# A graph network's aggregations: TensorE's counts raised by a drain instead of by the last product

## The chip, the cores and the metric

The kernel runs on one core of a Trainium2 chip. The metric is the device time of one execution in microseconds, without a profiler; three executions are listed, and their median counts. A profile is one further execution that the hardware profiler recorded.

## The reference, cut to what matters

Two layers of a graph network run over 6,250 nodes with 256 features and 100,000 edges that are sorted by destination. Layer 0 sums weighted neighbour rows, adds a linear attention, and ends in a routed feed-forward block of 32 experts. Layer 1 does two graph convolutions, a second mixer and a block with 64 slices in 8 heads. Everything is float32. The part that the change sits in is the neighbour sum, which is computed three times:

```python
msgs = edge_vals[:, None] * x[edge_src]
agg = jax.ops.segment_sum(msgs, edge_dst, num_segments=N)
# and twice, in the two convolutions of layer 1:
agg = jax.ops.segment_sum(norm[:, None] * xW[src], dst, num_segments=n_nodes)
```

## The kernel before, in words

**Stages.** The program runs stage after stage: setup, a front that normalises the rows, a first aggregation, two dense stages, routing with its experts, a second front, a second and a third aggregation, a small stage over heads and an output stage. In each stage every engine runs its own written-out list of instructions, and engines wait for one another by counts on semaphores.

**An aggregation** (`stage_aggregate`, run three times) takes the edges in 98 groups of 8 tiles with 128 edges each. GpSimd (POOL) issues one indirect gather per tile (`main_pool`, L1401), 784 per aggregation, into a ring of buffers `g` (4 groups deep in the first aggregation, 5 in the others). VectorE (DVE) builds for each tile a 128x128 matrix `m` that holds the edge's weight in the column of its destination (L1426; in the first aggregation also a matrix `eq` that counts edges, L1425). TensorE multiplies `m` with the gathered rows (`tile`, L1473) and sums the 8 tiles of a group in one of two PSUM banks. After every fourth tile the product raises the count `multiplied`. Three engines wait for it: POOL before it gathers into a buffer again, ScalarE (ACT) before it copies the finished bank to `s` (L1407), DVE before it overwrites `m`. TensorE then turns the copied window (`turn_window`, L1459 and L1461) and raises `window_turned`, and DVE adds it to `accT` (L1437).

**Order.** `main_pe` walks through rounds of 16 slots. A slot holds one tile; slots 3 and 11 also hold `turn_window` of the group before. 49 rounds have tiles; the loop has 50 rounds in the first aggregation, 53 in the second and 54 in the third.

**Side steps.** Into the slots of TensorE, ACT and DVE other work of the layer is set by a table (slot, list of steps, lag in rounds). `LinearAttention` runs beside the first aggregation: rows are turned (`turn_unit`, which calls `pe_turn`), multiplied by the key weights (`keys`, L612) and summed (`sums`, L644), 25 units in three units per two rounds; then, one unit a round, `turn`, `query` (L726), `norms` (L757), `mix` (L781) and `turn_back` (L802). `Between` runs beside the second: two units a round of `turn_unit` and `max_keys` (L940), then one a round of `turn_unit`, `keys` (L997) and `sum` (L1030), and in all rounds `product` (L1051) and `turn_t` (L1065). `Slices` runs beside the third: per round `turn2` (L1237), `mix` (L1251), `turn3` (L1290), `logits` (L1305), `sums` (L1340) and `turn_sw` (L1348). Each step ends by raising a count of its own with its last product. `pe_turn` is also called by the front, the routing and the second front (100 units in all).

A float32 product of 256 columns stands in the profile as two MATMUL rows.

Of the kernel before, what the change touches and what calls it, by code (L numbers as in the profile page):

```python
# [116 lines left out]
def pe_turn(kit, eng, bank, src, tiles, done):  # L117

    for j, w in enumerate(tiles):
        for c in range(C):  # L120
            ins = eng.transpose(bank[:, c * BODY + j * P:c * BODY + j * P + w],
                                src[0:w, j, c * P:(c + 1) * P], kit.ident[0:w, 0:w])
    ins.then_inc(done, 1)

# [361 lines left out]
class LinearAttention:  # L486
# [150 lines left out]
    def sums(self, u, tiles):  # L637
        pe, k = self.e_pe, self.k
        if u == 0:
            pe.wait_ge(self.one, self.XN)  # L640
        wait(pe, self.kf_done, u + 1)
        for j, w in enumerate(tiles):
            for c in range(C):
                ins = pe.matmul(k.bank[3 + c][:, 0:D + 1], self.kf[u % 2][0:w, j, c * P:(c + 1) * P], self.xn[u % self.XN][0:w, j, :],  # L644
                                start=(u == 0 and j == 0), stop=(u == self.UNITS - 1))
        ins.then_inc(self.summed, 1)

# [10 lines left out]
    def turn_A(self):  # L658
        pe, k = self.e_pe, self.k
        pe.wait_ge(self.a_read, 1)  # L660
        pe.wait_ge(self.xnT_done, self.UNITS)
        pe.wait_ge(self.z_done, self.UNITS)
        for c in range(C):
            for bank, o in ((2, 0), (5, 1)):
                pe.transpose(k.bank[bank][:, c * P:(c + 1) * P], self.A[:, c, o * P:(o + 1) * P], k.ident[:])
            ins = pe.transpose(k.bank[6][0:1, c * P:(c + 1) * P], self.A[:, c, D:D + 1], k.ident[:])
        ins.then_inc(self.a_turned, 1)

# [7 lines left out]
    def values(self):  # L676
        pe, k = self.e_pe, self.k
        pe.wait_ge(self.at_done, 1)
        for c in range(C):
            v = slice(D + c * P, D + (c + 1) * P)  # L680
            for o in range(C):
                pe.matmul(k.bank[4][:, c * P:(c + 1) * P], k.wkv0[:, o, v], self.AT[:, o, c * P:(c + 1) * P], start=(o == 0), stop=False)
            ins = pe.matmul(k.bank[4][:, c * P:(c + 1) * P], k.bkv0[0:1, v], self.srow[:, c, :], start=False, stop=True)
        ins.then_inc(self.kv_psum, 1)

# [7 lines left out]
    def mixer(self):  # L693
        pe, k = self.e_pe, self.k
        pe.wait_ge(self.masked, 1)
        for c in range(C):
            ins = pe.matmul(k.bank[6][:, c * D:(c + 1) * D], self.kvm[:, c, :], k.wo0[:, c, :], start=True, stop=True)
        ins.then_inc(self.m0_psum, 1)

# [18 lines left out]
    def query(self, v, _):  # L718
        if v >= self.UNITS:
            return  # L720
        pe, k, n = self.e_pe, self.k, sum(self.tiles(v))
        wait(pe, self.xnT_done, self.UNITS + v + 1)
        wait(pe, self.e_done, v)
        for o in range(C):
            for c in range(C):
                ins = pe.matmul(k.bank[3][:, o * BODY:o * BODY + n], k.wq0[:, c, o * P:(o + 1) * P], self.xnT[:, c, 0:n], start=(c == 0), stop=(c == C - 1))  # L726
        ins.then_inc(self.q_psum, 1)

# [20 lines left out]
    def norms(self, v, _):  # L749
        if v >= self.UNITS:  # L750
            return
        pe, k, n = self.e_pe, self.k, sum(self.tiles(v))
        wait(pe, self.q_done, v + 1)
        wait(pe, self.nr_done, 2 * v)
        pe.wait_ge(self.masked, 1)
        for c in range(C):
            ins = pe.matmul(k.bank[4][:, c * BODY:c * BODY + n], k.ks[:, c, :], self.q[v % 2][:, c, 0:n], start=True, stop=True)  # L757
        ins.then_inc(self.nrm_psum, 1)

# [12 lines left out]
    def mix(self, v, _):  # L772
        if v >= self.UNITS:
            return
        pe, k, n = self.e_pe, self.k, sum(self.tiles(v))
        wait(pe, self.qn_done, v + 1)
        wait(pe, self.s_done, v)
        pe.wait_ge(self.m0_done, 1)
        for o in range(C):
            for c in range(C):  # L780
                ins = pe.matmul(k.bank[5][:, o * BODY:o * BODY + n], k.m0[:, c, o * P:(o + 1) * P], self.q[v % 2][:, c, 0:n], start=(c == 0), stop=(c == C - 1))  # L781
        ins.then_inc(self.mix_psum, 1)

# [10 lines left out]
    def turn_back(self, v, _):  # L794
        if v >= self.UNITS:
            return
        pe, k = self.e_pe, self.k
        wait(pe, self.s_done, v + 1)
        wait(pe, self.half, v)
        for j, w in enumerate(self.tiles(v)):  # L800
            for c in range(C):
                ins = pe.transpose(k.bank[6][0:w, j * D + c * P:j * D + (c + 1) * P], self.s[:, c, j * P:j * P + w], k.ident[:])  # L802
        ins.then_inc(self.back, 1)

# [14 lines left out]
class Between:  # L819
# [109 lines left out]
    def max_keys(self, h):  # L929

        def step(i, w):
# [9 lines left out]
            ins.then_inc(self.key_psum, 1)  # L941
        return step
# [23 lines left out]
    def spread(self):  # L966
        pe, k = self.e_pe, self.k
        pe.wait_ge(self.mb_done, 1)
        for c in range(C):
            ins = pe.matmul(k.bank[4][:, c * P:(c + 1) * P], self.mb[:, c, :], k.ident[:], start=True, stop=True)  # L970
        ins.then_inc(self.mb_psum, 1)

# [15 lines left out]
    def keys(self, u, _):  # L988
# [9 lines left out]
        ins.then_inc(self.k_psum, 1)  # L998

# [19 lines left out]
    def sum(self, u, _):  # L1019
# [11 lines left out]
        ins.then_inc(self.summed, 1)  # L1031

# [13 lines left out]
    def product(self, i, w):  # L1046
# [3 lines left out]
        for c in range(C):  # L1050
            ins = pe.matmul(k.bank[6][0:w, 0:D], self.h[i % 2][:, c, 0:w], k.wg2[:, c, :], start=(c == 0), stop=(c == C - 1))  # L1051
        ins.then_inc(self.t_psum, 1)

# [7 lines left out]
    def turn_t(self, i, w):  # L1061
        pe, k = self.e_pe, self.k
        wait(pe, self.t_done, i + 1)
        for c in range(C):
            ins = pe.transpose(k.bank[6][:, c * P:c * P + w], self.t[i % self.T][0:w, c * P:(c + 1) * P], k.ident[0:w, 0:w])  # L1065
        ins.then_inc(self.t_turned, 1)

# [19 lines left out]
    def turn_A(self):  # L1087
# [6 lines left out]
        ins.then_inc(self.a_turned, 1)  # L1094

# [7 lines left out]
    def values(self):  # L1103
        pe, k = self.e_pe, self.k
        pe.wait_ge(self.lam_vec, 5)
        for c in range(C):
            for o in range(C):
                ins = pe.matmul(k.bank[4 + c][:, 0:D], self.AT[:, o, c * P:(c + 1) * P], k.wkv1[:, o, D:2 * D], start=(o == 0), stop=(o == C - 1))
        ins.then_inc(self.lam_psum, 1)

# [24 lines left out]
    def queries(self):  # L1135
# [5 lines left out]
        for c in range(C):  # L1141
            ins = pe.matmul(k.bank[4][:, 0:D], self.qb[:, c, :], self.lam[:, c, :], start=(c == 0), stop=(c == C - 1))
        ins.then_inc(self.mq_psum, 1)

# [8 lines left out]
class Slices:  # L1153
# [77 lines left out]
    def turn2(self, i, w):  # L1231
# [4 lines left out]
        for c in range(C):  # L1236
            ins = pe.transpose(k.bank[2][:, c * P:c * P + w], self.xn[i % self.XN][0:w, c * P:(c + 1) * P], k.ident[0:w, 0:w])  # L1237
        ins.then_inc(self.turned2, 1)

# [6 lines left out]
    def mix(self, i, w):  # L1246
# [5 lines left out]
        for c in range(C):  # L1252
            ins = pe.matmul(k.bank[2][0:w, c * P:(c + 1) * P], self.h[i % 2][:, c, 0:w], k.ident[:], start=False, stop=(c == C - 1))
        ins.then_inc(self.mixed, 1)

# [30 lines left out]
    def turn3(self, i, w):  # L1286
        pe, k = self.e_pe, self.k
        wait(pe, self.xn3_done, i + 1)
        for c in range(C):
            ins = pe.transpose(k.bank[2][:, c * P:c * P + w], self.xn3[i % self.LG][0:w, c * P:(c + 1) * P], k.ident[0:w, 0:w])  # L1290
        ins.then_inc(self.turned3, 1)

# [6 lines left out]
    def logits(self, i, w):  # L1299
# [4 lines left out]
        for c in range(C):  # L1304
            ins = pe.matmul(k.bank[6][0:w, :], self.xnT3[i % 2][:, c, 0:w], k.wxs[:, c, :], start=(c == 0), stop=(c == C - 1))  # L1305
        ins.then_inc(self.lg_psum, 1)

# [26 lines left out]
    def sums(self, i, w):  # L1334
# [6 lines left out]
        ins.then_inc(self.summed, 1)  # L1341

    def turn_sw(self, i, w):
# [3 lines left out]
        for q in range(HEADS * SLICES // P):  # L1347
            ins = pe.transpose(k.bank[6][:, q * P:q * P + w], lg[0:w, q * P:(q + 1) * P], k.ident[0:w, 0:w])  # L1348
        ins.then_inc(self.sw_turned, 1)

# [9 lines left out]
def stage_aggregate(nc, kit, a, d, table, side_of, count=False):  # L1360
# [6 lines left out]
    with Stage(nc, kit) as st:  # L1367
# [86 lines left out]
        def main_pe(pe):  # L1454
            def turn_window(n):
# [1271 lines left out]
```

## Time and profile before

| what | value |
|---|---|
| median of the runs, no profiler | 3846.96 us (3844.54 to 3854.53, 3 runs) |
| profiled execution, first to last instruction | 4334.5 us |
| PE (TensorE products) busy | 2842.8 us, 66% |
| POOL busy | 2524.5 us, 58% |
| DVE busy | 1865.2 us, 43% |
| ACT busy | 795.6 us, 18% |
| gathers (L1401) | 2352, of 128 rows each |

The profiled execution has only its span; no other time of it is known. The span is 487.5 us longer than the median of the runs. Busy time leaves out waits on semaphores and instructions that only a sequencer handles. The end of a product is modelled by the profiler, not observed; the start is recorded.

### The profile page before, as it was taken

The numbers are of one execution on the slowest core, as the hardware profiler recorded it, in microseconds if no ns is written. First come the engines' busy times: TensorE is split into PE (matmuls) and PEld (weight loads), VectorE is DVE, ScalarE is ACT, GpSimd is POOL, SyncE is SP. The second block draws the span as 40 slices with busy tenths as digits, with TensorE's granted clock in tenths as the row PEclk, the third lists the DMA queues.
The fourth block names the chain that finished last, engine by engine and source line by source line (L and its number), as shares of the span: only waits on it lengthen the run. The fifth ranks groups of instructions, "written<-read, shape, count | busy, mean of one in ns | idle before, by whom it ended". The sixth has DMA issues, their size and how long they took to land. (4 is left out here: it accounts for less than half of the span.)

```text
span 4334.5 us, 42515 instructions
## 1 busy us (share of the span) xinstructions
PE 2842.8 (66%) x12338; PEld 2151.9 (50%) x12338; DVE 1865.2 (43%) x5797; ACT 795.6 (18%) x1977; POOL 2524.5 (58%) x2689
## 2 busy tenths in 40 slices
PE   3577767777777566646656656555476767767678
PEld 2455545555544544435545545444354555555557
DVE  6343446666646823513322222222244444444443
ACT  1111101111113223301111111100022222232230
POOL 4666666666630533666666666665666666666601
PEclk9788879888888788978878778776788888888878
DMA  5333334444432466634333333332333333333305
GB/s 156 101 111 105 108 94 121 124 128 118 120 90 87 151 200 196 208 108 119 116 101 108 108 108 107 102 98 82 89 107 108 106 107 110 103 110 109 104 21 180
DMA packets 279543, 501.74 MB, mean 116 GB/s; under 512 B 59771, under 2 KB 179969, under 8 KB 279162
## 3 DMA queue, kind: packets, MB, share of 16 engines
q0 software_dynamic: 126240, 345.85, 27.7%
q1 hardware_dynamic: 135916, 139.10, 10.4%
q10 hardware_dynamic: 17136, 13.84, 1.0%
q8 instruction: 109, 1.79, 0.2%
q14 instruction: 142, 1.16, 0.1%
HBM read 419.12 MB, written 79.18 MB: 115 GB/s over the span
## 5 line engine op out<-in xcount | busy, mean ns | idle before, releaser
L1401 POOL DMA_INDIRECT g<-d_t,src_i x1568 | 1506.9, 961 | 806.4 <-issue 483.4
L1473 PE MATMUL bank<-g,m 128*128 128x256 f32 (+1 forms) x4704 | 1440.7, 438 | 94.3 <-issue 45.4
L1473 PEld LDWEIGHTS bank<-g,m 128*128 128x128 f32 x4704 | 943.0, 221 | 307.3 <-issue 141.2
L1401 POOL DMA_INDIRECT g<-d_xn,src_i x784 | 766.0, 977 | 389.2 <-issue 223.7
L1426 DVE TENSOR_SCALAR m<-iota,rel_f,ew_f 128x128 f32<-128x128 f32 x2352 | 702.0, 362 | 383.3 <-DMA d_xs<-zero 170.3
L1461 PE MATMUL bank<-ident,s 128*128 128x128 f32 x588 | 144.0, 334 | 438.3 <-ACT s L1407 390.2
L1437 DVE TENSOR_TENSOR accT<-bank,accT 128x256 f32 x294 | 121.9, 415 | 628.8 <-remote 269.8
L1407 ACT ACTIVATE s<-bank 128x256 f32<-128x256 f32 (+1 forms) x294 | 111.7, 380 | 1338.4 <-DMA nb<-d_deg 435.6
L1461 PEld LDWEIGHTS bank<-ident,s 128*128 128x128 f32 x588 | 86.3, 166 | 495.2 <-ACT s L1407 425.9
L1425 DVE TENSOR_SCALAR eq<-iota,rel_f 128x128 bf16<-128x128 f32 x784 | 227.5, 290 | 182.9 <-remote 140.3
L1435 DVE TENSOR_TENSOR dinv<-bank,dinv 2x128 f32 x98 | 27.1, 276 | 319.4 <-remote 310.0
L1008 DVE TENSOR_TENSOR side_z<-bank,bkv 128x512 f32<-128x512 f32 (+1 forms) x25 | 17.0, 681 | 293.0 <-issue 269.3
L1475 PE MATMUL bank<-ones_b,eq 128*128 128x1 bf16 x784 | 135.2, 172 | 8.1 <-issue 8.0
L174 POOL DMA_DIRECT2D out<-y x25 | 17.8, 714 | 197.3 <-DVE y L2575 197.3
L219 POOL TENSOR_TENSOR rsd<-ved,mhalf 128x2 f32<-128x2 f32 (+1 forms) x25 | 18.9, 756 | 182.8 <-DVE ved L213 182.6
L1305 PE MATMUL bank<-wxs,m 128*128 128x512 f32 (+1 forms) x196 | 121.6, 754 | 2.2 <-ACT m L1297 2.2
L612 PE MATMUL bank<-wkv,side_xnT 128*128 128x256 f32 (+1 forms) x196 | 67.4, 503 | 74.5 <-ACT side_xnT L596 45.7
L1237 PE MATMUL bank<-ident,side_xn 128*128 128x128 f32 (+1 forms) x98 | 25.3, 350 | 132.4 <-issue 132.4
L1251 PE MATMUL bank<-w1T,ks 128*128 128x256 f32 (+1 forms) x196 | 62.2, 446 | 75.0 <-issue 49.5
L2202 POOL DMA_DIRECT2D xt<-d_xs x80 | 43.0, 537 | 113.4 <-issue 110.0
L1340 PE MATMUL bank<-wg,side_lg 128*128 128x256 f32 (+1 forms) x392 | 96.3, 390 | 12.6 <-DVE side_lg L1332 10.8
L1475 PEld LDWEIGHTS bank<-ones_b,eq 128*128 128x128 bf16 x784 | 82.5, 105 | 43.7 <-issue 16.8
(386 smaller groups left out, 4235.9 us busy)
## 6 DMA issues: line engine op xcount, KB each, us to landing
g<-d_t,src_i POOLq DMA_INDIRECT x1568
side_xn<-d_xn SPq DMA_DIRECT2D x96, 256.0 KB
g<-d_xn,src_i POOLq DMA_INDIRECT x784
d_swT<-wkv SPq DMA_DIRECT2D x48, 256.0 KB
swT<-d_swT SPq DMA_DIRECT2D x24, 512.0 KB, 3.7
xt<-d_xs POOLq DMA_DIRECT2D x80, 128.0 KB, 2.9
d_ys<-y ACTq DMA_DIRECT2D x80, 128.0 KB, 2.5
x<-in_x SPq DMA_DIRECT2D x24, 256.0 KB, 2.8
```

The source lines that it names most:

```text
L612: ins = pe.matmul(k.bank[5][0:w, j * D:(j + 1) * D], self.xnT[:, c, j * P:j * P + w], k.wkv0[:, c, 0:D], start=(c == 0), stop=(c == C - 1))
L1251: pe.matmul(k.bank[2][0:w, 0:D], self.xnT[:, c, 0:w], k.mq[:, c, :], start=(c == 0), stop=False)
L1305: ins = pe.matmul(k.bank[6][0:w, :], self.xnT3[i % 2][:, c, 0:w], k.wxs[:, c, :], start=(c == 0), stop=(c == C - 1))
L1340: ins = pe.matmul(k.bank[3 + q // 2][:, q % 2 * D:(q % 2 + 1) * D], sw, self.xn3[i % self.LG][0:w, :], start=(i == 0 and q % 2 == 0), stop ...
L1401: pool.indirect_dma_start(g[n % RING][:, u, 0:D], None, table, bass.IndirectOffsetOnAxis(ap=k.src_i[:, t:t + 1], axis=0)).then_inc(gathere ...
L1407: act.activation(s[n % 2][:], k.bank[n % 2][:, 0:SW], ACT.Copy).then_inc(copied, 1)
L1425: dve.tensor_scalar(eq[r][:, u, :], k.iota[:], k.rel_f[:, t:t + 1], None, ALU.is_equal)
L1426: ins = dve.tensor_scalar(m[r][:, u, :], k.iota[:], k.rel_f[:, t:t + 1], k.ew_f[:, t:t + 1], ALU.is_equal, ALU.mult)
L1437: dve.tensor_tensor(at, chunks(k.bank[7]), at, ALU.add).then_inc(acc_added, 1)
L1461: ins = pe.transpose(k.bank[7][:, c * P:(c + 1) * P], s[n % 2][:, c * P:(c + 1) * P], k.ident[:])
L1473: ins = pe.matmul(b[:, 0:GW], m[o][:, u, :], g[r][:, u, :], start=(u == 0), stop=(u == GT - 1 and not count))
L1475: ins = pe.matmul(b[:, GW:SW], eq[o][:, u, :], k.ones_b[:, 0:1], start=False, stop=(u == GT - 1))
```

## The change

TensorE's counts in the aggregations, those of the side steps, and those of `pe_turn` wherever it is called, are no longer raised by the last product. A drain instruction follows that product on TensorE and raises the count in its place. The same line is changed in 27 places: in `pe_turn`; in `keys`, `sums`, `turn_A`, `values`, `mixer`, `query`, `norms`, `mix` and `turn_back` of `LinearAttention`; in `max_keys`, `spread`, `keys`, `sum`, `product`, `turn_t`, `turn_A`, `values` and `queries` of `Between`; in `turn2`, `mix`, `turn3`, `logits`, `sums` and `turn_sw` of `Slices`; in `turn_window` and `tile`. No product, load, buffer or wait changes. The setup, the dense stages, the expert, head and output stages keep their counts on products.

```diff
 def pe_turn(kit, eng, bank, src, tiles, done):
...
-    ins.then_inc(done, 1)
+    eng.drain().then_inc(done, 1)
...
     def keys(self, u, tiles):
...
-        ins.then_inc(self.key_psum, 1)
+        pe.drain().then_inc(self.key_psum, 1)
...
             def turn_window(n):
...
-                ins.then_inc(window_turned, 1)
+                pe.drain().then_inc(window_turned, 1)
 
             def tile(n, u):
...
                 if u % 4 == 3:
-                    ins.then_inc(multiplied, 1)
+                    pe.drain().then_inc(multiplied, 1)
```

## Rows read from the trace of the kernel before

**Rows 1.** The page's costliest groups: the gathers; busy us, mean ns, idle before.
```profile
L1401 POOL DMA_INDIRECT g<-d_t,src_i x1568 | 1506.9, 961 | 806.4 <-issue 483.4
...
L1401 POOL DMA_INDIRECT g<-d_xn,src_i x784 | 766.0, 977 | 389.2 <-issue 223.7
```

**Rows 2.** The gathers' line: durations, and POOL's idle time before them, by releaser.
```profile
L1401 POOL DMA_INDIRECT g<-d_t,src_i x1568: 942/946/1474, 1815.0 to 4114.0; - x196
...
  issue: 707.1, 2149
  remote: 146.4, 61
  DMA nb<-d_deg: 144.1, 51
  DMA d_xs<-zero: 142.7, 59
  PE bank L1473: 36.2, 22
  PE bank L1475: 19.2, 10
```

**Rows 3.** Timeline, a round's end in the second aggregation: start, us, [idle before <-releaser].
```profile
2398.74 1.89 PE L1473 MATMUL bank<-g,m 128*128 128x256 f32 x8
...
2401.33 0.59 PE L1473 MATMUL bank<-g,m 128*128 128x256 f32 x2
...
2405.80 0.95 POOL L1401 DMA_INDIRECT g<-d_t,src_i  x1 [0.30 <-issue]
...
2409.83 0.38 ACT L1407 ACTIVATE s<-bank 128x256 f32<-128x256 f32 x1 [12.52 <-DMA nb<-d_deg]
...
2410.06 0.95 POOL L1401 DMA_INDIRECT g<-d_t,src_i  x1 [3.32 <-DMA nb<-d_deg]
...
2410.26 0.69 PE L1461 MATMUL bank<-ident,s 128*128 128x128 f32 x2 [8.34 <-ACT s L1407]
```

**Rows 4.** Timeline of DVE in the third aggregation, after its last gather.
```profile
4159.09 0.69 DVE L1313 TENSOR_TENSOR side_lg<-bank,bxs 128x512 f32<-128x512 f32 x1 [2.78 <-PE bank L1305]
```

**Rows 5.** Timeline of PE in the third aggregation, after its last gather.
```profile
4122.47 0.38 PE L1461 MATMUL bank<-ident,s 128*128 128x128 f32 x2
...
4127.79 0.41 PE L1237 MATMUL bank<-ident,side_xn 128*128 128x128 f32 x2 [1.69 <-issue]
...
4142.65 0.41 PE L1237 MATMUL bank<-ident,side_xn 128*128 128x128 f32 x2 [1.69 <-issue]
...
4150.64 0.44 PE L1461 MATMUL bank<-ident,s 128*128 128x128 f32 x2
...
4152.34 0.44 PE L1290 MATMUL bank<-ident,wg 128*128 128x128 f32 x2 [0.82 <-DVE wg L1284]
...
4155.88 3.18 PE L1305 MATMUL bank<-wxs,m 128*128 128x512 f32 x4
...
4163.93 0.44 PE L1290 MATMUL bank<-ident,wg 128*128 128x128 f32 x2 [0.93 <-DVE wg L1284]
```

**Rows 6.** Timeline of PE in the first aggregation, two rounds of its second part.
```profile
915.50 0.68 PE L1473 MATMUL bank<-g,m 128*128 128x257 f32 x2
...
916.05 0.68 PE L1473 MATMUL bank<-g,m 128*128 128x257 f32 x2
...
916.60 0.64 PE L121 MATMUL bank<-ident,side_xn 128*128 128x128 f32 x4
...
920.85 1.99 PE L726 MATMUL bank<-side_xnT,wq 128*128 128x256 f32 x8 [1.30 <-ACT side_xnT L596]
...
931.93 0.66 PE L802 MATMUL bank<-ident,side_s 128*128 128x128 f32 x4 [1.23 <-ACT side_s L791]
...
933.67 1.11 PE L757 MATMUL bank<-side_q,ks 128*128 128x256 f32 x4
```

**Rows 7.** PE's groups by line and shape: the front's turned units.
```profile
L121 PE MATMUL bank<-ident,pxna 128*128 128x128 f32 x96 | 26.8, 435 | 39.2 <-DVE pxna L225 39.2
```

More of the change, by code:

```diff
@@ L645, in sums @@
                                 start=(u == 0 and j == 0), stop=(u == self.UNITS - 1))
-        ins.then_inc(self.summed, 1)
+        pe.drain().then_inc(self.summed, 1)
     def read_A(self):
@@ L666, in turn_A @@
             ins = pe.transpose(k.bank[6][0:1, c * P:(c + 1) * P], self.A[:, c, D:D + 1], k.ident[:])
-        ins.then_inc(self.a_turned, 1)
+        pe.drain().then_inc(self.a_turned, 1)
     def copy_AT(self):
@@ L683, in values @@
             ins = pe.matmul(k.bank[4][:, c * P:(c + 1) * P], k.bkv0[0:1, v], self.srow[:, c, :], start=False, stop=True)
-        ins.then_inc(self.kv_psum, 1)
+        pe.drain().then_inc(self.kv_psum, 1)
     def mask(self):
@@ L697, in mixer @@
             ins = pe.matmul(k.bank[6][:, c * D:(c + 1) * D], self.kvm[:, c, :], k.wo0[:, c, :], start=True, stop=True)
-        ins.then_inc(self.m0_psum, 1)
+        pe.drain().then_inc(self.m0_psum, 1)
     def copy_m0(self):
@@ L726, in query @@
                 ins = pe.matmul(k.bank[3][:, o * BODY:o * BODY + n], k.wq0[:, c, o * P:(o + 1) * P], self.xnT[:, c, 0:n], start=(c == 0), stop=(c == C - 1))
-        ins.then_inc(self.q_psum, 1)
+        pe.drain().then_inc(self.q_psum, 1)
     def exp(self, v, _):
@@ L757, in norms @@
             ins = pe.matmul(k.bank[4][:, c * BODY:c * BODY + n], k.ks[:, c, :], self.q[v % 2][:, c, 0:n], start=True, stop=True)
-        ins.then_inc(self.nrm_psum, 1)
+        pe.drain().then_inc(self.nrm_psum, 1)
     def normalise(self, v, _):
@@ L781, in mix @@
                 ins = pe.matmul(k.bank[5][:, o * BODY:o * BODY + n], k.m0[:, c, o * P:(o + 1) * P], self.q[v % 2][:, c, 0:n], start=(c == 0), stop=(c == C - 1))
-        ins.then_inc(self.mix_psum, 1)
+        pe.drain().then_inc(self.mix_psum, 1)
     def add_bias(self, v, _):
@@ L802, in turn_back @@
                 ins = pe.transpose(k.bank[6][0:w, j * D + c * P:j * D + (c + 1) * P], self.s[:, c, j * P:j * P + w], k.ident[:])
-        ins.then_inc(self.back, 1)
+        pe.drain().then_inc(self.back, 1)
     def sum(self, v, _):
@@ L940, in step @@
                     ins = pe.matmul(k.bank[3][:, o * BODY:o * BODY + n], k.wkv1[:, c, o * P:(o + 1) * P], self.xnT[:, c, 0:n], start=(c == 0), stop=(c == C - 1))
-            ins.then_inc(self.key_psum, 1)
+            pe.drain().then_inc(self.key_psum, 1)
         return step
@@ L970, in spread @@
             ins = pe.matmul(k.bank[4][:, c * P:(c + 1) * P], self.mb[:, c, :], k.ident[:], start=True, stop=True)
-        ins.then_inc(self.mb_psum, 1)
+        pe.drain().then_inc(self.mb_psum, 1)
     def shift(self):
@@ L997, in keys @@
                 ins = pe.matmul(k.bank[3][0:w, j * D:(j + 1) * D], self.xnT[:, c, j * P:j * P + w], k.wkv1[:, c, 0:D], start=(c == 0), stop=(c == C - 1))
-        ins.then_inc(self.k_psum, 1)
+        pe.drain().then_inc(self.k_psum, 1)
     def add_bias(self, u, _):
@@ L1030, in sum @@
                 ins = pe.matmul(k.bank[4 + c][:, 0:D + 1], self.z[0:w, j, c * P:(c + 1) * P], self.xn[(self.KEYS + u) % self.XN][0:w, j, :], start=(u == 0 and j == 0), stop=last)
-        ins.then_inc(self.summed, 1)
+        pe.drain().then_inc(self.summed, 1)
     def scale(self, i, w):
@@ L1051, in product @@
             ins = pe.matmul(k.bank[6][0:w, 0:D], self.h[i % 2][:, c, 0:w], k.wg2[:, c, :], start=(c == 0), stop=(c == C - 1))
-        ins.then_inc(self.t_psum, 1)
+        pe.drain().then_inc(self.t_psum, 1)
     def scale_t(self, i, w):
@@ L1065, in turn_t @@
             ins = pe.transpose(k.bank[6][:, c * P:c * P + w], self.t[i % self.T][0:w, c * P:(c + 1) * P], k.ident[0:w, 0:w])
-        ins.then_inc(self.t_turned, 1)
+        pe.drain().then_inc(self.t_turned, 1)
     def own(self, i, w):
@@ L1093, in turn_A @@
                 ins = pe.transpose(k.bank[2 + o][:, c * P:(c + 1) * P], self.A[:, c, o * P:(o + 1) * P], k.ident[:])
-        ins.then_inc(self.a_turned, 1)
+        pe.drain().then_inc(self.a_turned, 1)
     def copy_AT(self):
@@ L1108, in values @@
                 ins = pe.matmul(k.bank[4 + c][:, 0:D], self.AT[:, o, c * P:(c + 1) * P], k.wkv1[:, o, D:2 * D], start=(o == 0), stop=(o == C - 1))
-        ins.then_inc(self.lam_psum, 1)
+        pe.drain().then_inc(self.lam_psum, 1)
     def moments(self):
@@ L1142, in queries @@
             ins = pe.matmul(k.bank[4][:, 0:D], self.qb[:, c, :], self.lam[:, c, :], start=(c == 0), stop=(c == C - 1))
-        ins.then_inc(self.mq_psum, 1)
+        pe.drain().then_inc(self.mq_psum, 1)
     def copy_mq(self):
@@ L1237, in turn2 @@
             ins = pe.transpose(k.bank[2][:, c * P:c * P + w], self.xn[i % self.XN][0:w, c * P:(c + 1) * P], k.ident[0:w, 0:w])
-        ins.then_inc(self.turned2, 1)
+        pe.drain().then_inc(self.turned2, 1)
     def copy_xnT2(self, i, w):
@@ L1253, in mix @@
             ins = pe.matmul(k.bank[2][0:w, c * P:(c + 1) * P], self.h[i % 2][:, c, 0:w], k.ident[:], start=False, stop=(c == C - 1))
-        ins.then_inc(self.mixed, 1)
+        pe.drain().then_inc(self.mixed, 1)
     def combine(self, i, w):
@@ L1290, in turn3 @@
             ins = pe.transpose(k.bank[2][:, c * P:c * P + w], self.xn3[i % self.LG][0:w, c * P:(c + 1) * P], k.ident[0:w, 0:w])
-        ins.then_inc(self.turned3, 1)
+        pe.drain().then_inc(self.turned3, 1)
     def copy_xnT3(self, i, w):
@@ L1305, in logits @@
             ins = pe.matmul(k.bank[6][0:w, :], self.xnT3[i % 2][:, c, 0:w], k.wxs[:, c, :], start=(c == 0), stop=(c == C - 1))
-        ins.then_inc(self.lg_psum, 1)
+        pe.drain().then_inc(self.lg_psum, 1)
     def below_max(self, i, w):
@@ L1340, in sums @@
             ins = pe.matmul(k.bank[3 + q // 2][:, q % 2 * D:(q % 2 + 1) * D], sw, self.xn3[i % self.LG][0:w, :], start=(i == 0 and q % 2 == 0), stop=last and q % 2 == 1)
-        ins.then_inc(self.summed, 1)
+        pe.drain().then_inc(self.summed, 1)
     def turn_sw(self, i, w):
@@ L1348, in turn_sw @@
             ins = pe.transpose(k.bank[6][:, q * P:q * P + w], lg[0:w, q * P:(q + 1) * P], k.ident[0:w, 0:w])
-        ins.then_inc(self.sw_turned, 1)
+        pe.drain().then_inc(self.sw_turned, 1)
     def copy_swT(self, i, w):
```

## The prediction

> **What bounds the kernel now.** I read the page's groups first, then the gathers' line, then the timeline of one round. The reader should see that POOL's gathers fill the aggregations: 2352 of them take 1506.9 + 766.0 = 2272.9 us [rows 1], and nearly all are followed by the next after a pause of 0.30 us that waits for nothing [rows 3]. One gather costs 0.946 us at the median [rows 2], so the stream's pace is 0.946 + 0.30 = 1.25 us, and the 16 gathers of a round take 20.0 us whatever TensorE does.
>
> On top of this pace stand POOL's waits, all for `multiplied`: 146.4 + 144.1 + 142.7 + 36.2 + 19.2 = 488.6 us in 203 waits [rows 2]. Less the ordinary 0.30 us in each (61 us) that is 428 us. What the view names as releaser (a DMA of another stage, "remote") is not it: it found no product that ended shortly before. The timeline shows why. The tile that raises `multiplied` for the bank is the first of the four in the row at 2398.74, so it is over by about 2399.3; TensorE's last products end at 2401.92 and it then waits for ACT; yet ACT starts its copy at 2409.83 and POOL resumes at 2410.06 [rows 3]. The count arrived 10 us after the recorded end of its product. After the last gather of the third aggregation this is gone: the logits' products end at 4155.88 + 3.18 = 4159.06 [rows 5] and DVE starts at 4159.09 [rows 4].
>
> So there are two readings of the 428 us. Either TensorE's counts are late in every execution while gathers run, or they are late only under the profiler. The times decide between them as far as they can. Gathers that took longer than the median add 2272.9 - 2352 x 0.946 = 48 us. The profiled span without both is 4334.5 - 428 - 48 = 3858.5 us, and the runs take 3847.0 without a profiler. I take it that the runs are already bound by POOL's bare pace and have hardly any of these waits. The sum below is therefore made on 3847.0 and not on the span, and every price is of a round of 20.0 us that POOL sets.
>
> **What one drain costs TensorE.** No drain stands in the trace of before. It keeps the next product from entering until the last one is through. Two products take 0.59 us and eight 1.89 [rows 3]: 0.217 us for each further one, so 0.59 - 2 x 0.217 = 0.16 us are the tail that the next product otherwise covers. A restart has its price too: two turns take 0.44 us after an idle stretch and 0.38 in a stream [rows 5], which is 0.06; and from the end of ACT's copy (2409.83 + 0.38 = 2410.21) to TensorE's start at 2410.26 [rows 3] it is 0.05. Together 0.27; with something for the instruction itself I take 0.30 us. The lower bound is the tail alone, 0.16. The upper bound gives the drain an execution as long as POOL's pause between gathers, the nearest row of a sequencer's own time: 0.27 + 0.30 = 0.57. I stay near the low end, because three of the four parts are read from TensorE itself.
>
> **The change part by part.** In each aggregation 196 drains raise `multiplied` and 98 `window_turned`, six per round. The side steps add, per round: 4.5 in the first part of `LinearAttention` (three steps for 1.5 units), 5 in its second; 6, then 5 in `Between`; 6 in `Slices`. With 100 turned units outside, and steps that run once, about 1,700 drains.
>
> Now TensorE's round against POOL's 20.0. First aggregation, second part: a tile takes 916.05 - 915.50 = 0.55 us [rows 6], 16 of them 8.8; six turns of the windows at 0.12 (four in 0.64 less the tail, [rows 6]) 0.7; the side steps, each row less its tail, 0.48 + 1.83 + 0.95 + 0.50 [rows 6] and 1.83 for `mix`, which has the eight products of `query`: 5.6. Sum 15.1, and 11 drains make it 18.4. First part: 8.8 + 0.7 + 1.5 x (0.48 + 1.83 + 1.83) = 15.7, and 10.5 drains make it 18.9. Second aggregation: 32 products at 0.217, windows 0.5 and side steps of at most 5.5: 12.9, with 12 drains 16.5. Third: a round without gathers takes 4142.65 - 4127.79 = 14.86 us [rows 5], waits included, with 12 drains 18.5. All lie below 20.0. POOL's gathers cover the drains in all 147 rounds, with 1.1 us to spare at the tightest; without this cover 1,700 x 0.30 us would be some 510 us.
>
> Where a count is raised, it comes 0.2 to 0.3 us later than a prompt product's would. Behind it wait ACT's copies, DVE's next matrices and POOL's gather into the freed buffer; the ring is 4 or 5 groups deep, some 40 us of gathers, so POOL does not feel this.
>
> What is not covered lies where no gathers run. The third aggregation closes with four rounds of side steps, 4163.93 - 4152.34 = 11.6 us each [rows 5], 6 drains in each: 7 us if all lie on the chain, and I take half, since DVE and ACT stand in it too. The second closes with three rounds of two drains, 2 us. Of the turned units outside, three groups of four wait for DVE's normalised rows, as the front's does for 39.2 us [rows 7]; the fourth and the steps that run once I price at 3 us. Nothing of this can gain. Together +9 us, with bounds of 0 and 20: 3847 + 9 = **3856 us**. No change is what this measurement can't tell, 0.3% or 11.5 us, and the forecast lies inside it.
>
> **Where the skill says otherwise.** The row shows a count 10 us behind the modelled end of its product [rows 3]. The Trainium skill, PSUM — Partial Sum Buffer, section "Engine vs sequencer instructions", says that an update on an engine's instruction fires when that instruction completes, and that a drain waits until the engine is fully idle. By that rule the products themselves complete late, the trace's modelled ends are wrong, and each drain holds TensorE until then. The out-of-gather row (0.03 us) agrees with the rule; whether it holds among gathers no row shows. It is the last of the rivals.
>
> **The rivals.**
> - *TensorE becomes the bound of the first aggregation: slower.* The two waits for ACT in its round, 1.30 and 1.23 us [rows 6], stand beside the products; if they stay although counts are prompt in the runs, the round is 18.4 + 2.5 = 20.9, up to 21.4 in the first part. 0.9 to 1.4 us over POOL's pace in 49 rounds is 44 to 69 us: about 3910. It decides from a drain price of 0.22 us on with these waits, of 0.45 without. At 0.57 us it is 15.1 + 6.3 + 2.5 = 23.9, +190 us, and the third aggregation with 21.7 adds 83. For it: the small margin. Against it: these waits are probably children of late counts.
> - *The late counts are in the runs too, and the drains end them: faster.* All 428 of 4334.5 us is 9.9%, so 3847 x 0.90 = 3467; a residue that is left in the runs gives less, down to 1%. For it: POOL, ACT and TensorE all resume on a TensorE count. Against it: the arithmetic of 3858.5 against 3847.
> - *The drain does not do it:* the count comes as late as before. As POOL's pace rules the runs, the time is that of the forecast, and it is counted there.
> - *Products do complete late among gathers, in the runs too: far slower.* Each round's `multiplied` drain would hold TensorE for the 10 us seen; over 147 rounds 1,500 us, some 5,300 in all. Against it: again the arithmetic.
>
> **How the numbers follow.** Forecast case 0.60, of which 0.46 end within 0.3%, 0.10 above (ends dearer than 11.5 us) and 0.04 below. TensorE bound 0.26; late counts cured 0.10; late products 0.04. Faster 0.04 + 0.10 = 0.14, same 0.46, slower 0.10 + 0.26 + 0.04 = 0.40. The likeliest case has the range 3840 to 3875. The range for 8 in 10 takes in the smaller cures and most of the TensorE-bound case: 3800 to 3960. It leaves out the full cure, the dearest drains and the late products.
>
> **What the profile of the changed kernel would show.** Right: POOL's gathers still at 1.25 us and most of the span; TensorE's gaps after each fourth tile near 0.3 us; about 1,700 drains. If only the profiler makes counts late, its span may move far either way while the runs don't. Wrong: gaps of 0.5 us or more, POOL waiting for TensorE in the first aggregation with TensorE busy; or runs that fall along with POOL's waits, which would say that the 428 us were real.

## The result: slower by 0.66%

The changed kernel takes 3873.96 us (median of 4 runs, 3870.41 to 3878.2), the kernel before 3847.99 in runs beside it (4 runs, 3844.54 to 3854.53). The ratio is 1.0066 with a 95% interval of 1.0053 to 1.0079: 26 us longer, near 20 at the least.

The profiled execution of the changed kernel has a span of 3876.7 us, and its run took 3878.2. The page's groups and the gathers' line answer to [rows 1, 2]:

```profile
L1401 POOL DMA_INDIRECT g<-d_t,src_i x1568 | 1513.0, 965 | 515.7 <-issue 499.5
...
L1401 POOL DMA_INDIRECT g<-d_xn,src_i x784 | 760.1, 970 | 244.7 <-issue 241.3
```

```profile
  issue: 740.8, 2288
  PEq L1477: 19.5, 64
who waited for it (us, times):
  PE bank L1473: 421.2, 294
```

The 488.6 us in 203 waits of [rows 2] are gone. The 64 waits left for a drain ("PEq" is TensorE's sequencer, L1477 the drain behind a tile) are 0.30 us each, POOL's ordinary pause, so POOL waits for nothing at all; TensorE's products wait for POOL, 421 us. The counts come promptly too. In the second aggregation, three rows show a stretch of products and what the drain behind them releases:

```profile
1947.21 1.99 PE L1473 MATMUL bank<-g,m 128*128 128x256 f32 x8 [0.34 <-DMA g<-d_t,src_i]
...
1949.26 0.38 ACT L1407 ACTIVATE s<-bank 128x256 f32<-128x256 f32 x1 [4.07 <-PEq L1477]
1949.26 2.14 DVE L1426 TENSOR_SCALAR m<-iota,rel_f,ew_f 128x128 f32<-128x128 f32 x8 [1.49 <-PEq L1477]
```

The products end at 1949.20, ScalarE and VectorE start at 1949.26. In [rows 3] the same step lay some 10 us behind. Yet the time rose: the experiments show that those 10 us were not in the runs.

TensorE pays. First aggregation, second part, the counterpart of [rows 6]:

```profile
923.40 0.64 PE L802 MATMUL bank<-ident,side_s 128*128 128x128 f32 x4
924.11 0.70 PE L1473 MATMUL bank<-g,m 128*128 128x257 f32 x2
924.65 0.17 PE L1475 MATMUL bank<-ones_b,eq 128*128 128x1 bf16 x1
925.05 0.27 PE L1459 MATMUL bank<-ident,s 128*2 128x128 f32 x1 [0.23 <-issue]
```

In a stream four turns took 0.47 us from start to start: in the kernel before, this row follows the one at 916.60 in [rows 6].

```profile
917.07 0.60 PE L1473 MATMUL bank<-g,m 128*128 128x257 f32 x2
```

With the drain behind them they take 924.11 - 923.40 = 0.71: 0.24 us more. From the tile's last product at 924.65 to the next at 925.05, with a wait behind the drain, it is 0.40; where no drain stands the same step is 0.03 (926.15 to 926.18 in this round). That is 0.37 us. Of this, 0.23 is a gap that the profile puts down to no other engine ("issue").

### The profile page after: what moved, and what is told of

Its sections match the earlier page's. It is cut to its first block and busy times, and to the rows that moved or that the text cites. A ratio compares the mean times of both kernels' runs of the same rounds, so it can differ in the third digit from the quotient of the medians.

```text
span 3876.7 us, 44221 instructions
## 1 busy us (share of the span) xinstructions
PE 2978.0 (77%) x12338; PEld 1998.0 (52%) x12338; DVE 1885.5 (49%) x5797; ACT 795.3 (21%) x1977; POOL 2524.7 (65%) x2689
## 3 DMA queue, kind: packets, MB, share of 16 engines
q1 hardware_dynamic: 135916, 139.10, 11.6%
## 5 line engine op out<-in xcount | busy, mean ns | idle before, releaser
L1473 PE MATMUL bank<-g,m 128*128 128x256 f32 (+1 forms) x4704 | 1497.3, 439 | 535.8 <-DMA g<-d_t,src_i 294.9
L1473 PEld LDWEIGHTS bank<-g,m 128*128 128x128 f32 x4704 | 820.5, 203 | 1050.1 <-issue 666.1
L1461 PE MATMUL bank<-ident,s 128*128 128x128 f32 x588 | 124.7, 296 | 46.7 <-issue 46.5
L174 POOL DMA_DIRECT2D out<-y x25 | 17.8, 714 | 180.5 <-DVE y L2575 180.5
L1461 PEld LDWEIGHTS bank<-ident,s 128*128 128x128 f32 x588 | 66.9, 147 | 130.4 <-issue 129.9
L1305 PE MATMUL bank<-wxs,m 128*128 128x512 f32 (+1 forms) x196 | 118.7, 737 | 13.8 <-issue 10.8
L1356 ACT ACTIVATE wkv<-bank 128x128 f32<-128x128 f32 (+1 forms) x196 | 51.4, 277 | 262.6 <-PEq L1349 262.6
L1340 PE MATMUL bank<-wg,side_lg 128*128 128x256 f32 (+1 forms) x392 | 96.7, 391 | 3.8 <-DVE side_lg L1332 3.5
L1475 PEld LDWEIGHTS bank<-ones_b,eq 128*128 128x128 bf16 x784 | 80.0, 102 | 25.1
L2586 PE MATMUL bank<-wkv,swT 128*128 128x256 f32 (+1 forms) x392 | 86.6, 385 | 8.2 <-DMA swT<-d_swT 8.2
L2260 DVE COPY xT<-bank 128x256 f32<-128x256 f32 x80 | 33.9, 424 | 117.8 <-PE bank L2228 117.8
L1275 ACT ACTIVATE side_sd<-side_mv,eps 128x1 f32<-128x1 f32 (+1 forms) x49 | 14.4, 294 | 368.5 <-DVE side_mv L1269 368.5
L2586 PEld LDWEIGHTS bank<-wkv,swT 128*128 128x128 f32 (+1 forms) x392 | 75.5, 193 | 19.7 <-DMA swT<-d_swT 9.1
```

The costliest lines, as they stand in the source:

```text
L1356: ins = act.activation(self.swT[i % 2][:, q, 0:w], self.k.bank[6][:, q * P:q * P + w], ACT.Copy, accum_out=self.k.norms[:, q, i:i + 1])
L1473: ins = pe.matmul(b[:, 0:GW], m[o][:, u, :], g[r][:, u, :], start=(u == 0), stop=(u == GT - 1 and not count))
L1475: ins = pe.matmul(b[:, GW:SW], eq[o][:, u, :], k.ones_b[:, 0:1], start=False, stop=(u == GT - 1))
L2586: ins = pe.matmul(k.bank[4 + u.n % 4][0:w, j * D:(j + 1) * D], swT[u][:, j, c * P:c * P + w], k.mout[:, c, :], start=(c == 0), stop=(c == ...
```

## The experiments

Each ratio is to runs of the kernel before on the same chip (medians 3846.7 to 3849.0). `up` stands at all the places where the change puts a drain; the round of an aggregation is `NOW[0]`, which is None outside `main_pe`, and `NOW[1]` is the number of the aggregation. `NG // 2` is 49, so rounds from there on hold no tiles. The lines are cut at "...":

```
-            pe.drain().then_inc(...)
+            up(pe, ins, ...).then_inc(...)
+def up(eng, ins, part): return eng.drain() if NOW[0] is None else ins      # e1_outside
+... if part in ('tile', 'window') else ins                                 # e2_main
+... if NOW[0] is not None and NOW[0] >= NG // 2 else ins                   # e3_closing
+... if NOW[0] is not None and NOW[0] < NG // 2 else ins                    # e4_body
+... if NOW[0] is not None and NOW[0] < NG // 2 and NOW[1] == 3 else ins   # e6_third
```

What came out (median us of the runs; the other columns are from the one profile of each kernel). A stream is the time from the first gather of an aggregation to the end of its last; its excess is the gathers' busy time less 784 x 0.946 = 741.7 us. "Second front" is from its own first gather (L2333) to the first gather of the second aggregation, "closing" from the end of the third aggregation's last gather to the first step of the next stage:

| kernel | run | ratio, interval | 1st stream, excess | 3rd stream, excess | second front | closing |
|---|---|---|---|---|---|---|
| before, second profile | 3842.6 | one run | 997.3, 17.1 | 991.2, 10.9 | 111.9 | 54.2 |
| changed | 3874.0 | 1.0066, 1.0053 to 1.0079 | 998.6, 18.4 | 1003.3, 22.9 | 116.9 | 64.1 |
| e1_outside | 3851.8 | 1.0009, 1.0000 to 1.0018 | 999.4, 19.2 | 989.9, 9.6 | 115.6 | 54.1 |
| e2_main | 3861.8 | 1.0034, 1.0023 to 1.0045 | 1001.0, 20.9 | 1000.2, 19.9 | 111.9 | 56.5 |
| e3_closing | 3858.1 | 1.0027, 1.0018 to 1.0037 | 998.5, 18.4 | 989.9, 9.6 | 112.0 | 59.0 |
| e4_body | 3858.7 | 1.0023, 1.0014 to 1.0031 | 995.5, 15.3 | 1003.9, 23.6 | 112.0 | 55.9 |
| e6_third | 3865.9 | 1.0035, 1.0024 to 1.0047 | 1001.2, 20.9 | 1004.4, 24.1 | 112.4 | 56.4 |
| e7_one_input | 3860.0 | 1.0026, 1.0016 to 1.0036 | 994.9, 14.7 | 988.9, 8.7 | 117.0 | 64.9 |
| e8_one_input_products | 3844.8 | 0.9991, 0.9982 to 1.0000 | 998.0, 17.8 | 986.3, 6.1 | 112.0 | 54.2 |
| e9_psum | 3831.9 | 0.9959, 0.9945 to 0.9973 | 990.9, 10.8 | 984.2, 3.9 | 112.3 | 54.3 |
| e10_psum_drains | 3851.1 | 1.0007, 0.9997 to 1.0016 | 987.1, 6.9 | 989.5, 9.2 | 117.0 | 59.6 |
| e11_double | 3867.4 | 1.0052, 1.0038 to 1.0065 | 1001.6, 21.4 | 991.2, 10.9 | 118.2 | 65.0 |
| e12_both | 3868.4 | 1.0055, 1.0041 to 1.0069 | 992.5, 12.3 | 1003.5, 23.2 | 115.4 | 64.0 |

**Where do the 26 us lie?** The first four runs put the drains in some of the places each: outside (e1), behind tiles and windows (e2), in the rounds without gathers (e3) and in those with them (e4). e1, e3 and e4 together are the whole change.

> Drains only in the 100 turned units of the front, the routing and the second front; all counts inside the aggregations are raised by products as before. Theory A (the 26 us lie where no gathers run: in these stages and in the rounds after the last gather): 3853 us, +5, the 5 us by which the second front is longer in the changed kernel's profile. Theory B (the 26 us lie among the gathers, which the drains stretch although POOL shows no wait): 3848, no change. Profile: still late counts and a span near 4330, since nothing inside the aggregations is changed.

> Drains only behind the tiles (588) and the turned windows (294) of the aggregations. Theory A: +1 to +2 us, 3850, since only the last groups of each aggregation stand after the last gather. Theory B: about half of the change's cost, 3860, as 6 of about 11 drains per round are kept. Profile: six drains a round are enough to bring the span near the run's time, as with the whole change.

> Drains only in the rounds of the aggregations that hold no tiles (from the 50th on). Theory A: +8 to +20 us, 3856 to 3868, most of what the change costs, 6 us of it read from the third aggregation's closing rounds. Theory B: below +4, 3848 to 3852.

> Drains only in the 49 rounds of each aggregation that hold tiles; none outside and none in the closing rounds: about 1,500 of the change's 1,706 drains. Theory A: 3849, no change that can be measured, with POOL's gathers covering all of them, and a profile whose span is close to the run's time. Theory B: 3868 to 3874, all or nearly all of the change's cost.

Neither theory holds alone. By the ratios the turned units outside cost about 3 us, the rounds without gathers 10, and the rounds with gathers 9, though no gather waits in them. Of the 10, the profile of e3_closing shows 4.8 in the third closing and 1.3 between the second and the third stream; the rest it doesn't place. What the profile of e4_body shows of the 9 lies in the third stream. e1_outside misses its expected span: with the aggregations' bodies as in the kernel before, its span and that of e3_closing are 3848.4 and 3853.0 us, within 2 us of their profiled executions' times.

> The kernel before, unchanged, profiled a second time. Theory A (the waits for `multiplied`, 428 us, belonged to that one profiled execution): the aggregations here are as in the two kernels with few drains just run, whose spans of 3848.4 and 3853.0 us equal their runs, so the span is 3840 to 3855 us, POOL never waits and the three gather streams take about 999, 986 and 990 us. Theory B (the waits belong to this kernel under the profiler): span 4300 to 4370 us again, the streams about 1149, 1131 and 1138.

Span 3841.1 us, run 3842.6, and POOL waits for nothing:

```profile
L1401 POOL DMA_INDIRECT g<-d_t,src_i x1568: 944/946/1479, 1654.2 to 3649.0; - x196
L1401 POOL DMA_INDIRECT g<-d_xn,src_i x784: 942/946/1521, 108.2 to 1104.5; - x196
its engine sat idle before it (us, times) until:
  issue: 738.3, 2298
  PE bank L1473: 10.4, 34
  PE bank L1475: 6.1, 20
```

Theory A: the late counts of [rows 2, 3] belonged to that one profiled execution, not to the kernel and not to every profile of it. The change had nothing to cure. What made that one execution late stays open.

> Drains in the third aggregation alone, and there only while gathers run (rounds 0 to 48); products raise every other count. Theory A (the drains cost the third stream of gathers by themselves): that stream takes 1000 to 1005 us against 990, the other two stay at 999 and 985, the run is +12 us, about 3859, ratio 1.003. Theory B (the stream is longer because what ran before it shifted the phase): the third stream stays at 990 or moves by less than 4 us, the run is within 4 us of the kernel before, 3843 to 3851.

Theory A in place and roughly in size: the ratio is 1.0035, though the median of 3865.9 lies 7 us above the 3859 expected, and the third stream is at 1004.4 us, 13 over the second profile of before. The first stream has no drains here and still stands at 1001.2, 4 us over that profile: that much it varies without any drain. The third varies less in the three profiles that have no drain in it and the old steps (989.9 to 991.2).

**Why does a stream lengthen in which no gather waits?** Its pauses are 0.30 us as before; the gathers themselves are longer. In the changed kernel, third aggregation, first POOL's row, then VectorE's of the same time:

```profile
2774.20 0.95 POOL L1401 DMA_INDIRECT g<-d_t,src_i  x1 [0.30 <-issue]
2775.45 1.23 POOL L1401 DMA_INDIRECT g<-d_t,src_i  x1 [0.30 <-issue]
...
2774.45 0.69 DVE L1315 TENSOR_REDUCE side_mx<-side_lg 128x8 f32<-128x512 f32 x1
2775.17 0.69 DVE L1317 TENSOR_TENSOR side_lg<-side_lg,side_mx 128x512 f32<-128x512 f32 x1
```

The gather at 2774.20 ends beside a reduction with one operand and takes 0.95 us. That at 2775.45 starts while L1317 reads two operands from SBUF and ends at 2776.68, 0.82 us after L1317 (2775.86). In three such meetings of this kernel and two of the second profile of before (gathers of 1.23 to 1.46 us) this distance is 0.82 to 0.83 us. The whole third aggregation says the same. In the changed kernel 34 gathers start at least 0.05 us after L1317 or L1332 (another step with two SBUF operands) began and with more than 0.13 us of it to come: all end 0.82 to 0.83 us after that step. 57 others overlap such a step but start before it or at most 0.03 us after its start, and none takes more than 0.97 us. I read this as follows: the gather does its first 0.946 - 0.82 = 0.13 us, is held until VectorE's step is over, and goes on; where the gather was first it is not held. As a round is 16 gathers, a step that falls on a gather falls on one round after round. The Trainium skill, SBUF — State Buffer, section "Who interferes with whom", says that a VectorE instruction with two SBUF inputs contends with a GpSimd instruction that reads SBUF, and that a reduction never does; these rows agree. The next runs test it.

```
 # e7_one_input (all drains), e8_one_input_products (none): class Slices
-        dve.tensor_tensor(self.h..., k.accT[:, :, at], over_halves(k.dinv[:, at], w), ALU.mult)
+        dve.tensor_scalar(self.h..., k.accT[:, :, at], k.bg2c[:, 0:1], None, ALU.add)
-        dve.scalar_tensor_tensor(out=x3, in0=x3, scalar=k.mean2..., in1=chunks(k.bmq)...)
+        dve.tensor_scalar(x3, x3, k.mean2[0:w, i:i + 1], None, ALU.add)
-        dve.tensor_tensor(heads(lg), heads(lg), over(mx), ALU.subtract)
+        dve.tensor_scalar(lg[0:w, :], lg[0:w, :], k.eps[0:w, :], -4.0, ALU.min, ALU.max)
-        dve.tensor_tensor(heads(lg), heads(lg), over(self.tot), ALU.mult)
+        dve.tensor_scalar(lg[0:w, :], lg[0:w, :], self.tot[0:w, 0:1], None, ALU.mult)
```

> All the drains of the change, and in `Slices` the four VectorE steps with two operands in SBUF replaced by steps of the same shape with one: the factor 1/sqrt(deg) of `scale`, the bias row of `combine`'s second step, the largest logit in `below_max` and the heads' own sums in `weights` are left out. Theory A (a gather that starts while VectorE reads two SBUF operands is held until that step ends, and the drains moved those steps onto the gathers): the time of the third stream's gathers above 0.946 us each falls from 22.9 us to 3 to 6, the stream from 1003 to 983 to 987 us, the run to about 3857 (3874 less 17). Theory B (the drains lengthen the gathers in another way, by TensorE's later reads or the transfers): the sum stays at 18 to 23 us and the run at about 3873.

> The same four VectorE steps with one SBUF operand, and no drain anywhere: products raise all counts as in the kernel before. Left out are the same factor, bias row, largest logit and sums. Theory A: the gathers' sum above 0.946 us falls from 9.6 to 3 to 6 us, the third stream from 990 to 983 to 987 us, the run is about 3842 (3847 less 5), and the kernel with the drains stands only 13 to 16 us above it (second front 5, closing rounds 8) in place of 26. Theory B: the third stream stays at 990, the run at 3847, and the distance of the two stays at 26 us.

The third stream falls to 988.9 and 986.3 us, and the two kernels stand 15.3 us apart in place of 26. The excess stays a little above what was expected (8.7 and 6.1 us): the new steps with one SBUF operand hold gathers too, but for less, in e7_one_input's third stream 42 gathers by 5.2 us together beside L1317, L1332 and L1222. One doubt is left: the new steps are also shorter, about 0.50 us (L1317 505 ns, L1332 497 ns on the page) against 0.69. The next two runs keep the steps' length and the whole computation.

```
 # e9_psum (no drains), e10_psum_drains (all): an operand in PSUM
+        self.mx = [k.bank[5][:, HEADS * j:HEADS * (j + 1)] for j in range(2)]      # Slices
+        self.tot = k.bank[5][:, 2 * HEADS:3 * HEADS]
+        k.bmq = k.bank[5][:, D:2 * D]
+        nr = halves(k.bank[4][:])[:, :, 0:n]           # LinearAttention: reciprocals in place
+        act.activation(k.bank[3]..., k.bank[3]..., ACT.Exp, ...)        # after the Relu
+        dve.tensor_tensor(back, back, self.x..., ALU.add)   # back = bank 6, then xm = back + xn
-        waits of norms, query, turn_back: nr_done, e_done, half
+        waits of norms, query, turn_back: qn_done, q_done, xm_done
```

> No drains, and the whole computation with six VectorE steps changed so that one of their two operands lies in PSUM: in `LinearAttention` the reciprocals, the exponentials and the half sums stay in their banks, in `Slices` the largest logits, the heads' sums and the bias row move into the unused bank 5. Theory A (gathers are held by VectorE steps with two SBUF operands): the first stream's gathers above 0.946 us each fall from 17 us to 8 to 10 and the stream from 997 to 988 to 991, the third from 10 us to 4 to 6 and from 990 to 985 to 987; the run is 3833 to 3840, faster than the kernel before by 0.2 to 0.4%. Theory B (the earlier fall in the run with one-operand steps came from their shorter time of 0.49 us in place of 0.69): the streams stay at 997 and 990 and the run at 3843 to 3850.

> The same six steps with an operand in PSUM, and all the drains of the change. Theory A: the third stream falls from 1003 us to 986 to 990, the first from 998.6 to 988 to 991, the run to 3846 to 3852, some 13 us above the same kernel without drains (the second front's 5 and the closing rounds' 8 remain). Theory B: the streams stay at 998 and 1003 and the run at about 3870.

Theory A both times. The same meeting in e10_psum_drains, POOL's rows and VectorE's:

```profile
2765.65 0.95 POOL L1401 DMA_INDIRECT g<-d_t,src_i  x1 [0.31 <-issue]
2766.90 0.95 POOL L1401 DMA_INDIRECT g<-d_t,src_i  x1 [0.30 <-issue]
...
2765.87 0.69 DVE L1315 TENSOR_REDUCE bank<-side_lg 128x8 f32<-128x512 f32 x1
2766.60 0.69 DVE L1317 TENSOR_TENSOR side_lg<-side_lg,bank 128x512 f32<-128x512 f32 x1
```

L1317 takes as long, the gather starts 0.30 us after it began (0.28 above), and takes 0.95 us in place of 1.23. Over this third aggregation 48 gathers start inside L1317 or L1332, and none takes more than 0.96 us. More than half of the excess left, 5.1 of 9.2 us, is beside L1222, which keeps two SBUF operands. The windows of the three streams (length, gathers' busy time), e10_psum_drains and then the changed kernel:

```profile
106.40:1093.70 987.30, 748.52 (x784) 0.95 0.44 131
1652.80:2640.10 987.30, 748.52 (x784) 0.92 0.42 124
2662.40:3652.10 989.70, 750.90 (x784) 0.95 0.41 123
```

```profile
106.90:1105.80 998.90, 760.10 (x784) 0.96 0.44 129
1663.10:2650.30 987.20, 748.43 (x784) 0.91 0.43 124
2670.60:3674.00 1003.40, 764.61 (x784) 0.92 0.41 121
```

With the drains in, the six edits take 11.6 us from the first stream and 13.7 from the third. In the third only operands change; in the first three waits of TensorE move as well, so that its share is less clean. e9_psum, the same without drains, is the fastest kernel of the study: 3831.9 us, by the ratios 0.41% under the kernel before and 1.1% under the changed one (0.9959 / 1.0066). Its third stream and its run lie a little under what was expected. The drains cost it 19 us (3851.1 - 3831.9), where 13 were expected.

**What of a drain costs, the held TensorE or the later count?**

```
+def up(eng, ins, part): return (eng.drain(), eng.drain())[1]     # e11_double
+def up(eng, ins, part): return (eng.drain(), ins)[1]             # e12_both: the product raises the count
```

> Two drains in a row at every place of the change, the second raises the count. Theory A (a drain's price of 0.244 us is the products' tail and the restart, which the first one has paid): the second adds 0.02 to 0.1 us, TensorE's rounds stay below POOL's 20.0 us, the run is 3874 to 3884. Theory B (each drain has its own price of about 0.24 us): TensorE's rounds of the first aggregation come to about 18.4 + 11 x 0.24 - 11 x 0.06 = 20.4 us, which binds them and adds some 20 us there, the second front gains another 2 x 25 x 0.24 = 12, the closing rounds 8: about 3915.

> A drain after the last product at every place of the change, but the product raises the count as in the kernel before: TensorE is held as long, no count comes later. Theory A (what costs in the second front and in the closing rounds is the count that comes 0.24 us later on a chain of TensorE, ScalarE and VectorE; TensorE itself has room): the second front is back at 112 us, the closing rounds at 45 to 47, the run at 3847 to 3862 according to how the third stream's gathers meet VectorE's steps. Theory B (the held TensorE costs): second front 117, closing rounds 53, the run at 3870 to 3876.

A second drain costs little, Theory A: the gap behind a tile grows from 0.23 to 0.31 us. The run falls 7 us under its range, and the third stream, at 991.2 us, is 12 shorter than in the changed kernel. TensorE still does not bind: POOL's 33 waits for it are 10.1 us, 0.31 each. With doubled drains the third stream is shorter than with single ones, so its length is not a price per drain.

In e12_both my Theory A fell, and Theory B comes close: the run is 1.6 us under its range. The second front stays at 115.4 us and the closing at 64.0, although no count waits for a drain. It is mostly the hold that costs; of the second front's 5.0 us it leaves 3.5. The second front, PE rows of one unit: before (its second profile), changed, e12_both.

```profile
1573.99 0.66 PE L121 MATMUL bank<-ident,pxne 128*128 128x128 f32 x4 [1.00 <-DVE pxne L225]
1574.48 0.60 PE L121 MATMUL bank<-ident,t 128*128 128x128 f32 x4
1574.92 1.89 PE L2391 MATMUL bank<-wg,xnT 128*128 128x256 f32 x8
1577.82 0.66 PE L121 MATMUL bank<-ident,pxne 128*128 128x128 f32 x4 [1.01 <-DVE pxne L225]
```

```profile
1581.39 1.97 PE L2391 MATMUL bank<-wg,xnT 128*128 128x256 f32 x8 [0.26 <-issue]
1583.19 0.60 PE L121 MATMUL bank<-ident,pxne 128*128 128x128 f32 x4
1584.37 0.66 PE L121 MATMUL bank<-ident,t 128*128 128x128 f32 x4 [0.57 <-ACT t L2375]
1585.25 1.97 PE L2391 MATMUL bank<-wg,xnT 128*128 128x256 f32 x8 [0.23 <-issue]
```

```profile
1571.96 1.97 PE L2391 MATMUL bank<-wg,xnT 128*128 128x256 f32 x8 [0.21 <-issue]
...
1574.93 0.66 PE L121 MATMUL bank<-ident,t 128*128 128x128 f32 x4 [0.57 <-ACT t L2375]
1575.80 0.67 PE L2391 MATMUL bank<-wg,xnT 128*128 128x256 f32 x2 [0.21 <-issue]
```

Before, a unit takes 3.83 us and TensorE waits 1.01 of it for normalised rows; the last two units, with no gather of their own beside them, take 3.40. With drains all steady units take at least 3.86 (1585.25 - 1581.39), with the wait now for ScalarE: TensorE and ScalarE in turn have become the bound. From the first turn of `t` to L2391 it was 0.44 us and is 0.88. In e12_both it is 0.87: the same.

The closing rounds, PE rows of one round, before and changed, the counterpart of [rows 5]:

```profile
3662.97 0.51 PE L1237 MATMUL bank<-ident,side_xn 128*128 128x128 f32 x2 [2.81 <-issue]
3663.28 3.57 PE L1305 MATMUL bank<-wxs,m 128*128 128x512 f32 x4
3666.68 1.03 PE L1251 MATMUL bank<-w1T,ks 128*128 128x256 f32 x4
...
3671.73 0.44 PE L1290 MATMUL bank<-ident,wg 128*128 128x128 f32 x2 [1.41 <-DVE wg L1284]
```

```profile
3689.54 0.66 PE L1237 MATMUL bank<-ident,side_xn 128*128 128x128 f32 x2 [3.23 <-ACT m L1297]
3690.43 3.75 PE L1305 MATMUL bank<-wxs,m 128*128 128x512 f32 x4 [0.23 <-issue]
3694.41 1.49 PE L1251 MATMUL bank<-w1T,ks 128*128 128x256 f32 x4 [0.23 <-issue]
...
3698.64 0.63 PE L1348 MATMUL bank<-ident,side_lg 128*128 128x128 f32 x4 [0.23 <-issue]
3699.35 0.43 PE L1290 MATMUL bank<-ident,wg 128*128 128x128 f32 x2
```

From L1237 to L1290 it was 8.76 us and is 9.81, and the whole round, from one L1290 to the next, went from 12.0 to 13.5: products that ran into each other now stand 0.23 us apart. But the gaps are not all of it: L1251 takes 1.49 us in place of 1.03, L1305 3.75 in place of 3.57. TensorE's granted clock over the closing is 0.74, in the second profile of before 0.81: more of it passes at the lower level, 1.2 GHz, and less at 2.4. e10_psum_drains has the same drains there:

```profile
3666.66 0.66 PE L1237 MATMUL bank<-ident,side_xn 128*128 128x128 f32 x2 [3.23 <-ACT m L1297]
3667.55 3.16 PE L1305 MATMUL bank<-wxs,m 128*128 128x512 f32 x4 [0.23 <-issue]
3670.93 1.10 PE L1251 MATMUL bank<-w1T,ks 128*128 128x256 f32 x4 [0.23 <-issue]
...
3675.60 0.44 PE L1290 MATMUL bank<-ident,wg 128*128 128x128 f32 x2 [0.19 <-DVE wg L1284]
```

With the same gaps its round takes 8.94 us. The two kernels with drains in the closing and a granted clock of 0.82 over it, e3_closing and e10_psum_drains, close in 59.0 and 59.6 us; the four at 0.71 to 0.74 (changed, e7, e11, e12) take 64.0 to 65.0. So about 5 of the 9.9 us are there at the clock of before. The rest goes with the lower clock and, by 1 to 2 us, with the last turns of windows ahead of these rounds. TensorE idles about 3 us at the start of such a round with the drains and without; whether they bring the lower clock about, no run shows.

## Why the prediction was right and wrong

*The 428 us are not in the runs:* right, and shown (e5_before). The sum that it was argued from came out near the runs partly by luck. Of the 48 us of long gathers that it took off, some 33 (17.1 + 4.6 + 10.9) are in an undisturbed profile too; with them left in, 3858.5 becomes 3891, 50 us above the second profile's span. 29 of those 50 are the third closing, 83.4 us in the first profile and 54.2 in the second, which the sum left out.

*The gathers cover the drains in all 147 rounds:* right in that POOL never waits for TensorE, even with two drains at each place. This also settles the TensorE-bound rival and the one of products that complete late: both false. That this cover is free is the step that failed: the forecast has no term for the gather rounds, and took 1.25 us as the gathers' pace "whatever TensorE does". The pace depends on which VectorE step runs when a gather starts, and TensorE's counts release VectorE's steps. The third stream rose by 12.1 us (991.2 to 1003.3), all of it in gathers of over 0.946 us, 9.7 of it in gathers held by the four two-operand steps of `Slices` (17.1 us against 7.4). That the hold is VectorE's is shown by e9_psum and e10_psum_drains. That with drains more gathers meet these steps can be counted: 27 to 32 start inside one of the four, with more than 0.13 us of it to come, in the three profiles without drains in that stream (e5, e1, e3), 75 to 91 in the five with single ones and the old steps (changed, e2, e4, e6, e12). Why the drains shift the steps onto the gathers is not shown: with doubled drains it is 35 and 991.2 us, and the first stream ranged from 992.5 to 1001.6 us over the kernels with the old steps. How one would foresee it stays open.

*The drain's price:* 0.30 us, measured 0.24 without and 0.37 with a wait behind the drain. The tail was sized right; the restart of 0.06 + 0.05 was about right without a wait (a gap of 0.08) and too small with one (0.23). Its 0.06 rested on thin ground: two turns take 0.44 us also at 4150.64 in [rows 5], where no idle stretch stands before them.

*The uncovered ends:* +9 us forecast; two pairs of kernels that differ in the drains, in which the changed steps of `Slices` have at most one SBUF operand, stand 15.3 and 19.1 us apart. The third aggregation's closing is the term that was too small: 3.5 us forecast as half of the drains, 9.9 measured (54.2 to 64.1). In the closing round shown three of the six drains leave a gap of 0.23 us and two one of 0.08, so TensorE was on the chain more than half: with drains there and the clock of before the closing costs about 5 us. Another 3 go with products that ran longer at the lower clock, which no term foresaw (L1305, L1251 and L1340 after the first closing turn take 25.1 us in all, 21.9 in e3_closing). The windows' last turns, not counted either, are 2.2 us of the 9.9. The second front took 5.0 us against 3 for all turned units and single steps.

So 3856 lacked the third stream's 12 us and some 6 to 10 us of ends. The measured 3874 is at the very top of the range given for the forecast case, 3840 to 3875. That it lies inside is luck in so far as the sum has no term for the third stream's 12 us.

## What to carry to other kernels

A drain on TensorE costs its price only where TensorE stands on the chain, but there it cost 0.2 to 0.4 us here, mostly by breaking a stream of products and little by the later count; count such places before counting drains. Read the granted clock of a stretch before putting all of its growth down to the change. Where another engine's stream binds, do not treat its pace as a constant: look at its longest instructions and what ran beside them when they started. Before pricing a wait of hundreds of us, see whether span and run agree, and profile a second time.

## What the hardware showed unexpectedly

Of two profiled executions of the same kernel one had counts up to 10 us late and a span of 4334.5 us, the other had 3841.1.

A gather of GpSimd's queue that starts inside a VectorE step with two SBUF operands (L1317, L1332) ends 0.82 us after that step, up to 0.53 us late (1.48 us for the longest in the third aggregation of the second profile of before); one that starts before the step is not held. With one operand in PSUM the step takes as long and the gather 0.95 us. Moving six operands to PSUM was worth 15.6 us of 3847.5.
